# One core, two layers with attention and experts: another order in the first stage, a product in strips and tanh for sigmoid in the last, and a measurement moved

## The reference

```python
x = L0_attn_x                                   # (4, 1024, 256)
xn = _layernorm(x)
x = x + attention(xn)                           # one head, causal softmax
      + experts(xn)                             # 8 experts, top 2, 256 -> 1024 -> 256, relu
xn = _layernorm(x)
# linear attention, 16 heads of 16
q_feat, k_feat = elu(rope(q) / 4) + 1, elu(rope(k)) + 1
kv = einsum('bhtd,bhtv->bhdv', k_feat, v)
out = einsum('bhtd,bhdv->bhtv', q_feat, kv) / denom[..., None]
# channel mix
r = sigmoid(einsum('btc,dc->btd', xr, W_r))
out2 = r * einsum('btc,dc->btd', square(relu(k)), W_v)
return x + out @ W_out + out2
```

## Time and profile before

| | |
|---|---|
| median of 3 runs | 971.42 us (969.96 to 972.36) |
| profiled execution, its own time | 967.42 us |
| its span in the trace | 965.8 us |
| PE busy | 866.4 us, 90% |
| DVE busy | 674.6 us, 70% |
| ACT busy | 515.6 us, 53% |
| POOL busy | 190.9 us, 20% |
| granted clock of PE, mean | 0.965 |

### The profile page before, as it was taken

The page is one execution under the profiler, slowest core; times in us unless marked ns, Lnnn a source line. Parts: engine busy times, 40 slices in busy tenths (PEclk is TensorE's granted clock), DMA queues, the critical chain, the costliest instruction groups (busy, mean ns, idle before and its releaser), DMA issues. The chain is left out here.

```text
span 965.8 us, 16221 instructions
## 1 busy us (share of the span) xinstructions
PE 866.4 (90%) x5619; PEld 775.2 (80%) x5619; DVE 674.6 (70%) x1287; ACT 515.6 (53%) x907; POOL 190.9 (20%) x238
## 2 busy tenths in 40 slices
PE   4898430899899999999999999999989999999998
PEld 3687320788799989999998999999878787978877
DVE  7787100445657887878888787888487979799764
ACT  3642100333655565565656556565458867677581
POOL 1004777000000000000000000000613436163202
PEclk9999765799999999999999999999999999999999
DMA  8771445200744667656666765762301112021101
GB/s 267 265 260 60 147 147 177 79 1 1 260 132 144 212 209 240 201 176 236 225 198 205 256 201 174 239 213 76 93 23 31 58 45 77 13 84 46 43 1 44
DMA packets 93871, 134.24 MB, mean 139 GB/s; under 512 B 8608, under 2 KB 78688, under 8 KB 93824
## 3 DMA queue, kind: packets, MB, share of 16 engines
q1 hardware_dynamic: 85024, 107.80, 33.8%
q0 software_dynamic: 8800, 25.83, 8.1%
HBM read 98.22 MB, written 35.39 MB: 138 GB/s over the span
## 5 line engine op out<-in xcount | busy, mean ns | idle before, releaser
L1064 PE MATMUL ps<-w2h,hh 128*128 128x256 f32 x568 | 162.8, 287 | 0.0
L1204 ACT ACTIVATE h<-ps,b1T 128x512 f32<-128x512 f32 (+1 forms) x160 | 90.5, 588 | 132.7 <-PE ps L1066 132.5
L1066 PE MATMUL ps<-w2h,hl 128*128 128x256 f32 x568 | 160.7, 283 | 0.0
L1065 PE MATMUL ps<-w2l,hh 128*128 128x256 f32 x568 | 160.6, 283 | 0.0
L1309 DVE TENSOR_TENSOR hl<-h,hh 128x512 fp32r<-128x512 f32 x124 | 85.5, 689 | 66.1 <-ACT hh L1208 65.0
L1053 POOL DMA_DIRECT2D expert_out<-y x28 | 20.5, 733 | 476.5 <-DVE y L1268 476.5
L1064 PE MATMUL ps<-xTh,w1h 128*128 128x512 f32 (+1 forms) x320 | 110.6, 345 | 2.4 <-DVE xTl L1251 2.4
L1064 PEld LDWEIGHTS ps<-w2h,hh 128*128 128x128 f32 x568 | 108.7, 191 | 2.4 <-DVE hl L1309 0.2
L1065 PE MATMUL ps<-xTl,w1h 128*128 128x512 f32 (+1 forms) x320 | 110.6, 346 | 0.0
L1065 PEld LDWEIGHTS ps<-w2l,hh 128*128 128x128 f32 x568 | 108.7, 191 | 2.1
L1066 PE MATMUL ps<-xTh,w1l 128*128 128x512 f32 (+1 forms) x320 | 110.0, 344 | 0.0
(11 more groups left out here) (309 smaller groups left out, 2210.9 us busy)
## 6 DMA issues: line engine op xcount, KB each, us to landing
raw<-in_L_ffn_W SPq DMA_DIRECT2D x30, 1024.0 KB
raw_odd<-in_L_ffn_W SPq DMA_DIRECT2D x28, 1024.0 KB, 7.2
dispatched<-shared SPq DMA_DIRECT2D x1, 9088.0 KB, 32.1
expert_out<-y POOLq DMA_DIRECT2D x11, 512.0 KB, 3.6
rows<-dispatched SPq DMA_DIRECT2D x20, 256.0 KB, 3.4
shared<-in_L_ffn_b SPq DMA_DIRECT2D x9, 512.0 KB, 8.2
xn_rows<-raw SPq DMA_DIRECT2D x4, 1024.0 KB, 5.2
rows<-xn_rows SPq DMA_DIRECT2D x32, 128.0 KB
```

Of the source, the lines that this page charges most:

```text
L1064: pe.matmul(out, ah, bh, start=start, stop=False, skip_group_check=True)
L1065: pe.matmul(out, ah, bl, start=False, stop=False, skip_group_check=True)
L1066: return pe.matmul(out, al, bh, start=False, stop=stop, skip_group_check=True)
L1204: op = act.activation(h32[:, at, cols], ps[:, slot, cols], ACT.Relu, bias=s.b1T[:, ds(e * HC + w * tile.chunks + n, 1)])
```

## The change

In the first part `xn` gets three homes (sequence 2 in `s.shared[:, 1]`), so the wait for the turning of sequence 0 is left for sequence 3 alone. Unit 2 is normalized by ACT (`normalized`) with a scale and a shift that DVE makes (`shifts`). The fold of the weights and its copy move behind the routing of sequence 1. The lower parts of the first keys and of the fold move behind the last normalizing on DVE. The first softmax also waits for the stores from the third home.

In `body` the kv product is made in four strips of 32 columns against 33 columns of `v1`, each strip into its own 32 output partitions. The gate is a tanh of half the argument; W_v is halved, and `apply_gate` adds one before it multiplies. The measurement of the second half of the next sequence moves on DVE from before the first two gates to before the last two divisions, its `scales` behind them; on ACT its root moves between the `oT` copies and its normalizing behind them.

```diff
-        xn = s.raw[:, :].rearrange("p (u i d) -> p u i d", u=2, i=BT)
+        xn_homes = [s.raw[:, u * BT * D:(u + 1) * BT * D].rearrange("p (i d) -> p i d", i=BT) for u in range(2)]
+        xn_homes.append(s.shared[:, 1, :].rearrange("p (i d) -> p i d", i=BT))
...
             turn_tokens(1)
-            fold_weights()
             for b in range(2, B + 2):
                 if b < B:
                     turn_tokens(b)
                 if b <= B:
                     route(b - 1)
                 turn_logits(b - 2)
+                if b == 2:
+                    fold_weights()
...
+            def normalized(n):
+                b, tiles = UNITS[n]
+                act.wait_ge(shift_done, 1)
+                for t in tiles:
+                    op = act.activation(xn(b)[:, t % BT, :], x_tile(t), ACT.Identity,
+                                        bias=shift[:, t % BT:t % BT + 1], scale=rstd[:, t:t + 1])
+                op.then_inc(xn_ready, 1)
...
+            shifts(2)
+            statistics(3)
+            dve.wait_ge(xn_ready, 3)
+            normalize(3)
+            statistics(4)
+            normalize(4)
+            dve.wait_ge(xh_ready, 1)
+            V.tensor_tensor(xl[:, 0], xnT_early[:, :, 0:T], xh[:, 0].bitcast(F32), ALU.subtract
...
-        v1 = sb("v1", [P, BT, DC, P + 1])
+        Q, NQ = 32, P // 32
+        v1 = sb("v1", [P, BT, DC, NQ, Q + 1])
...
                     for i in range(BT):
-                        mm = pe.matmul(ps[:, 4 + c, 0:P + 1], feat[:, i, D + c * P:D + (c + 1) * P], v1[:, i, c, :],
-                                       start=(i == 0), stop=(i == BT - 1))
+                        for q in range(NQ):
+                            of = slice(D + c * P + q * Q, D + c * P + (q + 1) * Q)
+                            mm = pe.matmul(ps[q * Q:(q + 1) * Q, 4 + c, 0:Q + 1], feat[:, i, of], v1[:, i, c, q, :],
+                                           start=(i == 0), stop=(i == BT - 1))
...
-                    act.activation(gate[:, 2 * n:2 * n + 2, :], pair_of_tiles(ps[:, 4 + n, :]), ACT.Sigmoid
+                    act.activation(gate[:, 2 * n:2 * n + 2, :], pair_of_tiles(ps[:, 4 + n, :]), ACT.Tanh, scale=0.5
...
-                    V.tensor_tensor(at, pair_of_tiles(ps[:, (6 + n) % 8, :]), at, ALU.mult).then_inc(gated, 1)
+                    V.scalar_tensor_tensor(at, at, 1.0, pair_of_tiles(ps[:, (6 + n) % 8, :]), ALU.add, ALU.mult
+                                           ).then_inc(gated, 1)
...
                 if not last:
                     add_rows(b + 1, 1, 1)
                     scales(b + 1, 0)
-                    measure(b + 1, 1)
                 apply_gate(0)
                 apply_gate(1)
-                if not last:
-                    scales(b + 1, 1)
                 divide(0)
                 divide(1)
                 apply_gate(2)
                 apply_gate(3)
+                if not last:
+                    measure(b + 1, 1)
                 divide(2)
                 divide(3)
+                if not last:
+                    scales(b + 1, 1)
```

More of the change, by code:

```diff
@@ L165, in norm_route_attend @@
         unused = sb("unused_root", [P, 1])
+        shift = sb("shift", [P, BT])
         b1r = sb("b1r", [E * s.HC, P])
@@ L337, in turn_tokens @@
                         mm = pe.transpose(ps[:, q, i * P:(i + 1) * P],
-                                          xn[:, b % 2, half * 4 + i, c * P:(c + 1) * P], s.ident[:, :])
+                                          xn(b)[:, half * 4 + i, c * P:(c + 1) * P], s.ident[:, :])
                     mm.then_inc(turned, 1)
@@ L550, in _ @@
                 logits_out(b - 2)
+                if b == 2:
+                    act.wait_ge(folded, 1)
+                    act.activation(ah[:, :, :], ps[:, 7, :].rearrange("p (c d) -> p c d", c=DC), ACT.Copy,
+                                   scale=D ** -0.5).then_inc(ah_ready, 1)
             def project_hi(b, results):
@@ L581, in turned_hi @@
                                    ps[:, 4:6, :].rearrange("p h k -> p (h k)")[:, 0:n * P], ACT.Copy).then_inc(pT_hi, 1)
+                if first:
+                    act.wait_ge(xn_stored[1], 32)
                 softmax(0)
@@ L614, in statistics, with invert, shifts @@
                 op.then_inc(mv_done, 1)
+            def invert(n):
+                at = slice(UNITS[n][1][0], UNITS[n][1][-1] + 1)
+                dve.wait_ge(std_done, n + 1)
+                V.reciprocal(rstd[:, at], std[:, at]).then_inc(rstd_done, 1)
+                dve.wait_ge(rstd_done, n + 1)
+                return at
+            def shifts(n):
+                at = invert(n)
+                V.scalar_tensor_tensor(shift[:, :], mv[:, at, 0], -1.0, rstd[:, at], ALU.mult, ALU.mult
+                                       ).then_inc(shift_done, 1)
             def normalize(n):
                 b, tiles = UNITS[n]
-                dve.wait_ge(std_done, n + 1)
-                at = slice(tiles[0], tiles[-1] + 1)
-                V.reciprocal(rstd[:, at], std[:, at]).then_inc(rstd_done, 1)
-                dve.wait_ge(rstd_done, n + 1)
-                if b >= 2:
-                    dve.wait_ge(turned, 4 * (b - 1))
-                    dve.wait_ge(xn_stored[b % 2], 16)
+                invert(n)
+                if b == B - 1:
+                    dve.wait_ge(turned, 4)
+                    dve.wait_ge(xn_stored[0], 16)
                 for t in tiles:
-                    op = V.tensor_scalar(xn[:, b % 2, t % BT, :], x_tile(t), mv[:, t, 0:1], rstd[:, t:t + 1],
+                    op = V.tensor_scalar(xn(b)[:, t % BT, :], x_tile(t), mv[:, t, 0:1], rstd[:, t:t + 1],
                                          ALU.subtract, ALU.mult)
@@ L634, in _ @@
             statistics(2)
-            for n in range(2, len(UNITS)):
-                if n + 1 < len(UNITS):
-                    statistics(n + 1)
-                if n == len(UNITS) - 1:
-                    dve.wait_ge(xh_ready, 1)
-                    V.tensor_tensor(xl[:, 0], xnT_early[:, :, 0:T], xh[:, 0].bitcast(F32), ALU.subtract
-                                    ).then_inc(xl_ready, 1)
-                    dve.wait_ge(ah_ready, 1)
-                    V.scalar_tensor_tensor(al[:, :, :], ps[:, 7, :].rearrange("p (c d) -> p c d", c=DC), D ** -0.5,
-                                           ah[:, :, :].bitcast(F32), ALU.mult, ALU.subtract).then_inc(al_ready, 1)
-                normalize(n)
+            shifts(2)
[6 more added lines that the diff above has]
+            V.tensor_tensor(xl[:, 0], xnT_early[:, :, 0:T], xh[:, 0].bitcast(F32), ALU.subtract
+                            ).then_inc(xl_ready, 1)
+            dve.wait_ge(ah_ready, 1)
+            V.scalar_tensor_tensor(al[:, :, :], ps[:, 7, :].rearrange("p (c d) -> p c d", c=DC), D ** -0.5,
+                                   ah[:, :, :].bitcast(F32), ALU.mult, ALU.subtract).then_inc(al_ready, 1)
             steps = [0]
@@ L1850, in _ @@
             act.wait_ge(weights_turned, 1)
-            act.activation(wT[:, :, :, :].rearrange("p n c d -> p n (c d)"), ps[:, 4:7, :], ACT.Copy
+            act.activation(wT[:, 0:2].rearrange("p n c d -> p n (c d)"), ps[:, 4:6, :], ACT.Copy)
+            act.activation(wT[:, 2].rearrange("p c d -> p (c d)"), ps[:, 6, :], ACT.Copy, scale=0.5
                            ).then_inc(weights_ready, 1)
@@ L1930, in body @@
                 if not last:
-                    for u in range(2):
-                        deviation(b + 1, u)
-                        normalized(b + 1, u)
+                    deviation(b + 1, 0)
+                    normalized(b + 1, 0)
                 for m in range(4):
                     h, c = m // 2, m % 2
+                    if m == 2 and not last:
+                        deviation(b + 1, 1)
                     act.wait_ge(att_turned, 4 * b + m + 1)
                     act.activation(oT[:, c, h * HB:(h + 1) * HB], ps[:, 2 + c, :], ACT.Copy).then_inc(oT_ready, 1)
+                    if m == 3 and not last:
+                        normalized(b + 1, 1)
                 if not last:
```

40 lines of the change are left out of this document (21 added, 19 removed).

## The result

The changed kernel took 958.52 us (median of 4 runs, 956.88 to 960.52) where the kernel before took 970.69 (4 runs, 968.32 to 972.36) on the same chip: a ratio of 0.9877 with a 95% interval of 0.9846 to 0.9908. The profiled executions stand at 956.88 us (span 955.2) against 967.42 us (span 965.8), so 10.5 us apart. Forecast were 959.5 us and, between the profiled executions, 11.9 us.

The account below looks back on a forecast made before the run. PE, 90% busy, bounds the kernel; the scatter's end, set by its start, decides when PE is free again. 3.9 + 1.7 + 2.0 + 2.0 + 2.3 = 11.9 us off 967.42: 955.5; median 4.0 above: 959.5 us, range 955.5 to 968.5.

Parts of the forecast that it names:

- First part, 3.9 us: Layer-1 start: last normalizing on DVE ends at 30.0 instead of 33.87 us, moving the scatter's start and end 3.9 us sooner.
- The kv product, 1.2 us: PE in `body`: 128 instructions of 33 columns in four side-by-side strips take 1.2 us instead of 3.74.
- The size of a round: kv product: four strips' instructions of 33 columns take 28 ns together; 32 rounds 0.9 us, plus 0.3 to drain.
- The rival by the instruction: kv product: strips paced by the instruction still take 3.2 to 3.7 us, total 968.3 us; chance 15%.
- The slower rival, PE's sequencer: kv product: 128 instructions at 0.046 to 0.067 us take 5.9 to 8.6 us, total 978 to 988; chance 8%.
- Mixing sooner by 1.9, 2.1, 2.3 us: PE in `body`: value mixing starts sooner by 1.9 (b = 0), 2.1 (b = 1), 2.3 us (b = 3).
- PE waits for the four squares: `body`: behind the shorter product PE waits for ACT's squares, which end 1.28 us sooner without the table load.
- Passages 1.7, 2.0, 2.0 us: `body`: the next sequence starts sooner by 1.7 us for b = 0 and 2.0 for b = 1 and 2.
- Last sequence 2.3 us: `body`, b = 3: no passage to a next sequence, so it keeps its whole 2.3 us.
- The moved measurement: DVE in `body`: without the move DVE would be late for the quotients once mixing starts 2.1 us sooner.
- The crawl unchanged: PE, ACT and DVE crawl beside the scatter's transfers; taken as unchanged, PE resuming near 169 us instead of 173.
- the rival that the crawl swallows part of the gain: Beside the scatter: about 4 us more left undone at 169 us, only `body`'s 8.0 remains, 963.4 us; chance 15%.

Follow-up runs that it names:

- the run with eight in a row: Changed kernel with its 128 kv products ordered eight in a row in the same strip, not one in each strip in turn: 971.77 us.
- the second trace: The changed kernel again, no edit, on a chip where PE does not crawl beside the scatter: 892.22 us, 0.9878 of the kernel before.
- both later edits: Changed kernel, POOL's value-weight splitting held back, second scales one division earlier: 890.93 us; on the third chip with lower parts ahead of the third addition too: 960.65 us.
- the other two kernels there: Changed kernel with eight products in a row in the same strip, 971.77 us; changed kernel with two strips of 64 columns, 964.66 us.
- the last experiment: Changed kernel with value-weight splitting later, second scales one division earlier, and DVE's lower parts ahead of the third addition: 960.65 us, 0.9854 of the kernel before.

## Why the prediction was right, and where it was off

The forecast 959.5 us came out at 958.52, and `body`'s share came from the right causes. The sum of the terms, 11.9 us, was 1.4 us too large against the profiled executions, mostly in the first part and in the gap of the product; that the median still came within 1.0 us is luck (last point).

- **First part, 3.9 us.** It was 2.8 at the scatter's start and 3.2 at the start of `body` in this pair of traces. The step that was mis-sized: "DVE's reciprocal and normalizing (0.2 and 2.67) then end at 23.5". The normalizing took 3.63 us beside POOL's splitting, whose trigger on ACT the change had moved next to it; with the splitting moved away it took 2.68. All else in this term (ACT's eight by 20.33, the root by 20.5, PE's turning at 20.4 instead of 22.2, the two instructions hidden in DVE's pause, now 3.10 us) came as worked out.
- **The kv product, 1.2 us.** It took 1.30 us in one piece. That the overlap between strips is what makes it short, the run with eight in a row shows: without it 28 ns is the price of every instruction. The size of a round was put too low: 1.30 us less 0.20 for the last instruction leaves some 35 ns for each of 31 steps, not 28, so four strips in turn cost a quarter more than one alone. The drain of 0.20 instead of 0.3 us hid half of that. The rival by the instruction (968.3 us) falls here: 128 instructions in 1.30 us are 10 ns each. The Trainium skill's rule of about 60 cycles per matmul, on its page TensorEngine Tiling (Array Packing), section Performance Considerations (Instruction Overhead), an estimated 3.2 us for all, does not hold for four strips in turn. In one strip the 128 took 3.56 us, close to that estimate, but 33 columns at the rate of the whole array (0.11 us for 129) also give 28 ns each, so no run here tells the rule from the columns. The slower rival, PE's sequencer at 46 to 67 ns each, falls with it.
- **Mixing sooner by 1.9, 2.1, 2.3 us.** Counted from the sequence's start, as the prediction did, it is 2.05, 1.94 and (b = 3) 2.33 us less. For b = 0 the product itself starts 0.48 us sooner, since the wait for the gate (0.35 us in the earlier trace rows) is gone. "PE waits for the four squares" was true for b = 0 alone (0.8 us); from b = 1 on the squares ended first, 0.2 to 0.6 us before the mixing started, and what was missing for b = 1 was the gap in the product, absent on another chip (there 2.33).
- **Passages 1.7, 2.0, 2.0 us.** They kept 1.73, 1.61 and 1.79, and in the second trace, without the gaps in the product, 1.73, 1.99 and 2.01. The step held: the lower parts started on ACT's xh, as I had it. What I had not seen is that DVE's third addition ends only 0.2 to 0.4 us ahead of it, so that the queue takes over as soon as xh comes sooner.
- **Last sequence 2.3 us.** 2.24.
- **The moved measurement** I had treated as what keeps the mixing's gain. It is: without it the three passages keep next to nothing (2.7 us in all and not 7.4). On top of the other two it was worth most, 4.6 us, and I had no row of its price. What it brings by itself was not run.
- **The crawl unchanged.** This did not hold. PE ran on at 171.8 us and not at 169, and came to the experts 4.6 us sooner with a scatter that ended 2.55 sooner; then it lost 1.4 us on the way to `body`. That 3.2 were left is in part luck. On the third chip the same step went the other way: with both later edits the scatter ended 5.0 us sooner than in its kernel before, and PE came to the experts only 2.3 us sooner (246.87 and 249.13); in the other two kernels there it was 2.9 of 4.5 and 4.5 of 4.2. So the rival that the crawl swallows part of the gain is not refuted by one trace. For the gain as such the crawl is not needed: where it is absent, the change is worth 11.1 us all the same.
- **Between profiles and medians:** 10.5 us between the profiled executions, 12.2 us between the medians. The forecast took the kernel before's median to stand 4.0 us above its profiled execution; with the fourth run it stood 3.3 above, and the changed kernel's stands 1.6 above its own. That the sum missed by 1.4 us and the median by 1.0 in the other direction is the spread of the runs (about 4 us), not insight.

## What to carry to other kernels

A shorter step on the full engine pays only as far as the next late wait: here the shorter product alone is worth 1.4 us in `body`, the missing table load alone 0.1, both 2.7, and both with the measurement (and ACT's order) out of the way 7.4; so look for what is late next and move it in the same change. When a step moves, check what runs beside it on GpSimd at its new place. What is won ahead of a wait of PE can be given back by the granted clock behind it: here 0.6 of 0.6 us and 1.6 of 1.9. And cutting the block-diagonal product into strips of 32 columns paid only because consecutive instructions stand in different strips.

## What the runs showed of the hardware

- The same kernel takes 971 or 974 us on two measurements and 903 or 904 us on two others. Nearly all of the difference lies beside the 64 indirect transfers of the scatter (PE turned the experts' first rows at 243.39 us in the first trace and at 181.84 in the run with tanh alone, 61.5 of the 63 us by which `body` starts apart): PE was busy for 19.85 of 75 us at a granted clock of 0.61 in the earlier trace rows's dip, and for 74.84 of 75 us at 1.00 in the run with tanh alone, with POOL and the DMA share alike (57.90 and 58.85 us, 0.50 and 0.48). The cause is open.
- Without the crawl PE's granted clock was 0.57 to 0.72 over the 12 us behind its wait of 2.5 to 5.6 us for the experts' first rows, for the same work (five traces with the new first part). The stretch from there to `body` took 485.5 us at 0.72 and 487.2 at 0.57, in two kernels with the same list up to there.
- One POOL instruction of 1.28 us (128x512, to fp32r) beside eight DVE instructions stretched these from 2.67 to 3.63 us. A lower part of DVE (0.68 us) that started while POOL's addition ran took 1.55 to 1.77 us. One that already ran when POOL's addition started kept its 0.68, and the addition took 1.66 instead of 1.28. In the last experiment DVE's addition from PSUM (L2196) started beside POOL's and kept its 0.68. The splitting beside DVE's statistics, as in the kernel before, stretched nothing: 2.71 us there as elsewhere.
- Four strips in turn: 10 ns per instruction of 33 columns (1.30 us for 128). One strip eight times in a row: 28 ns. Two strips of 64 columns with 65: 33 ns. The recorded duration of one is about 0.2 us in all three.
